# Second cross-attention: probabilities transposed on VectorE in 32x32 blocks, values as four row tiles

## The chip, the cores and the metric

The kernel runs on one core of a Trainium2 chip. The metric is the device time of one execution in microseconds, the median of several runs. Lower is better.

## What is computed

Two layers of a perceiver (cross-attention, self-attention, feed-forward) over x of 128 batches, 32 queries and 128 features, with a context of 128 x 257 x 128. The change touches only the second layer's cross-attention:

```python
Q = (queries @ W_Q).reshape(b, sq, H, DK)      # b=128, sq=32, H=16, DK=64
K = (keys @ W_K).reshape(b, skv, H, DK)        # skv=257; keys = values = context
V = (values @ W_V).reshape(b, skv, H, DV)
scores = jnp.einsum('bqhd,bkhd->bhqk', Q, K)
scores = jnp.where(mask == 0, -jnp.inf, scores)
probs = jax.nn.softmax(scores * scaling, axis=-1)
attn = jnp.einsum('bhqk,bkhd->bqhd', probs, V).reshape(b, sq, H * DV)
return attn @ W_O
```

All of it is in f32. The kernel folds W_Q with W_K into `A` and W_V with W_O into `BH` (`c_B` in the rows), so that scores and values work on the raw context of 128 features.

## The kernel before

The program is a chain of phases, each over all the data; `phase_xattn1` (line 755) is the one here, its tiles and buffers named `c_...`. Its main part takes one batch a step, 128 steps, and a tile is four batches (32 x 4 = 128 rows of x). The engines run the same steps, each with its own written order, coupled by semaphores; `run` (line 888) unrolls the first 8 steps, loops over eight at a time, and unrolls the last. r is the step modulo 8, and what depends on it does so modulo 4.

TensorE in step g (`step`, line 985):
- scores of batch g (L962): four matmuls of 257 keys, one for each group of four heads, into banks `b_s`;
- values of batch g-2 (L981): the probabilities, keys on the partitions (`PT`), times the context `C` (two halves of 128 keys), 512 columns each, into bank `b_o`;
- queries (L946) for the next tile, a quarter in each step, into bank `b_q`;
- at r%4 = 1 a small matmul of the last key's probabilities (L997); at r%4 = 2 the output projection of a tile, 16 matmuls (L1007) and one of 64 rows (L1009), into free columns of `b_s[0]`;
- the turn of batch g-1's probabilities (L970): eight transposes of 128x128 into two banks `b_pt`.

A matmul of f32 stands in the trace as two loads and two matmuls, a transpose as one of each.

ScalarE: the exponentials of batch g-1 (L1038, four, each followed by a read of the sum), eviction of the values (L1044, `OT`), eviction of the queries (L1026, `QP`), and eviction of the first half of the turned probabilities (L1051). VectorE: mask and maximum for each of four head groups (L1072), the reciprocal, scaling of the probabilities by it (L1082), at r%4 = 1 the small tile `LT` (L1087), at r%4 = 2 the addition to X (L1092), and the second half of the turned probabilities (L1098). GpSimd copies the last key's columns. SyncE loads for each batch the transposed context `cT` and the context rows `C`, eight buffers each.

Waits that the prediction follows: scores at r%4 = 0 wait for all four query evictions of their tile (`q_ev`); the second head group's scores at r%4 = 2 wait for `LT` to be made (`l_ev`), whose source lies in the same bank; the first group's at r%4 = 3 wait for the addition to X (`y_ev`), again for the bank's sake.

Of the kernel before, what the change touches and what calls it, by code (L numbers as in the profile page):

```python
# [754 lines left out]
def phase_xattn1(nc, sh, ctx_rows, mask, w_q, w_k, w_v, w_o):  # L755
# [7 lines left out]
    with ExitStack() as ctx:  # L763
# [8 lines left out]
        C = sb("c_C", [P, NC_, 2, D])  # L772
# [5 lines left out]
        PT = sb("c_PT", [P, 2, 2, 4, P])  # L778
# [8 lines left out]
        b_pt = [psum("c_bp0"), psum("c_bp1")]  # L787
        b_o, b_q = psum("c_bo"), psum("c_bq")

        with ExitStack() as prep:  # L790
# [15 lines left out]

            phase_norm(nc, sh, "c_n_", loads, b_pt)
# [68 lines left out]
        c_in = [sem(f"c_c_in{i}") for i in range(NC_)]  # L876
        ct_in = [sem(f"c_ct_in{i}") for i in range(NC_)]
        vb_in = [sem(f"c_vb_in{i}") for i in range(2)]
        taken, last_cp, bm_ok = sem("c_taken"), sem("c_last_cp"), sem("c_bm_ok")
        q_ps, q_ev = sem("c_q_ps"), sem("c_q_ev")  # L880
        s_ps, s_mx, s_nmx, e_ok = sem("c_s_ps"), sem("c_s_mx"), sem("c_s_nmx"), sem("c_e_ok")
        rd_ok, n_ok, x_ok = sem("c_rd_ok"), sem("c_n_ok"), sem("c_x_ok")
        pt_ps, pt0_ev, pt1_ev = sem("c_pt_ps"), sem("c_pt0_ev"), sem("c_pt1_ev")
# [57 lines left out]
        def _(pe):  # L941
            def queries(tile, c):
# [22 lines left out]
            def turn_probs(s, pair):  # L965
                wait(pe, n_ok, 4 * (s.g - 1) + 2 * pair + 2)
                wait(pe, (pt0_ev, pt1_ev)[pair], s.g - 1)
                for c in range(2):
                    for k in range(2):
                        last = nc.tensor.transpose(b_pt[pair][:, (2 * c + k) * P:(2 * c + k + 1) * P],  # L970
                                                   PR[:, 1 - s.r % 2, 2 * pair + k, c * P:(c + 1) * P], sh.ident[:, :])
                last.then_inc(pt_ps, 1)

            def values(s):
                g, buf = s.g, (s.r - 2) % NC_
                pe.wait_ge(c_in[buf], 16 * (s.eights(-2) + 1))
                wait(pe, pt0_ev, g - 1)
                wait(pe, pt1_ev, g - 1)
                wait(pe, o_ev, g - 2)
                for c in range(2):  # L980
                    last = nc.tensor.matmul(b_o[:, :], C[:, buf, c, :], PT[:, s.r % 2, c, :, :],  # L981
                                            start=(c == 0), stop=(c == 1))
                last.then_inc(av_ps, 1)

            def step(s):
                g, r = s.g, s.r
                if s.on(0):
                    scores(s)
                if s.on(2):
                    values(s)  # L990
                if s.on(-4):
                    queries(s.tile + 1, r % 4)
                if r % 4 == 1 and s.on(5):
                    wait(pe, x_ok, 4 * s.fours(-5) + 4)
                    if s.on(0):
                        wait(pe, s_mx, 4 * g + 2)
                    nc.tensor.matmul(b_s[1][0:BPT * H, SPARE:SPARE + SQ], XL[:, (r - 5) // 4 % 2, :, :, :],  # L997
                                     sh.fold[:, :], start=True, stop=True).then_inc(l_ps, 1)
                if r % 4 == 2 and s.on(6):
                    t, tp = s.fours(-6), (r - 6) // 4 % 2  # L1000
                    wait(pe, o_ev, 4 * t + 4)
                    wait(pe, l_ev, t + 1)
                    pe.wait_ge(vb_in[tp], 16 * (s.eights(-6) + 1))
                    if s.on(0):
                        wait(pe, s_mx, 4 * g + 1)
                    for h in range(H):
                        nc.tensor.matmul(b_s[0][:, SPARE:SPARE + D], OT[:, tp, h, :, :], BH[:, h, :],  # L1007
                                         start=(h == 0), stop=False)
                    nc.tensor.matmul(b_s[0][:, SPARE:SPARE + D], LT[:, :, :], VB[:, tp, :], start=False, stop=True  # L1009
                                     ).then_inc(y_ps, 1)  # L1010
                if s.on(1):
                    turn_probs(s, 0)
                    turn_probs(s, 1)

            for c in range(4):
                queries(0, c)
# [3 lines left out]
        def _(act):  # L1020
            nc.scalar.activation(warm[:, :], sh.ident[:, 0:1], ACT.Exp)

            def queries(tile, par, c):
# [3 lines left out]
                                     b_q[:, :].rearrange("p (h b q) -> p h b q", h=4, b=BPT), ACT.Copy  # L1027
                                     ).then_inc(q_ev, 1)

            def step(s):  # L1030
                g, r = s.g, s.r
                par = r % 2
                if s.on(1):
                    wait(act, s_nmx, g)
                    wait(act, pt_ps, 2 * (g - 2))
# [5 lines left out]
                if s.on(2):  # L1041
                    wait(act, av_ps, g - 1)
                    wait(act, y_ps, s.fours(-2) - 1)
                    nc.scalar.activation(OT[:, (r - 2) // 4 % 2, :, (r - 2) % 4, :],  # L1044
                                         b_o[:, :].rearrange("p (h q) -> p h q", h=H), ACT.Copy).then_inc(o_ev, 1)
                if s.on(-4):
                    queries(s.tile + 1, 1 - r // 4 % 2, r % 4)
                if s.on(1):
                    wait(act, pt_ps, 2 * (g - 1) + 1)
                    wait(act, av_ps, g - 2)  # L1050
                    nc.scalar.activation(PT[:, 1 - par, :, 0:2, :].rearrange("p c k q -> p c (k q)"),  # L1051
                                         b_pt[0][:, :].rearrange("p (c k) -> p c k", c=2), ACT.Copy).then_inc(pt0_ev, 1)
# [6 lines left out]
        def _(dve):  # L1059
# [4 lines left out]
            def step(s):  # L1064
# [12 lines left out]
                if s.on(1):  # L1077
# [17 lines left out]
                if s.on(1):  # L1095
                    wait(dve, pt_ps, 2 * g)
                    wait(dve, av_ps, g - 2)
                    nc.vector.tensor_copy(PT[:, 1 - par, :, 2:4, :].rearrange("p c k q -> p c (k q)"),  # L1098
                                          b_pt[1][:, :].rearrange("p (c k) -> p c k", c=2)).then_inc(pt1_ev, 1)
# [1349 lines left out]
```

## Time and profile before

| | us |
|---|---|
| median of 3 runs (2770.66 to 2772.89) | 2771.66 |
| profiled execution, time | 2771.93 |
| profiled execution, span | 2770.2 |
| scores of this phase, first to last start | 1068.2 to 1873.8 |

Over the whole span TensorE is busy 82% of the time, VectorE 60%, ScalarE 56%, GpSimd 17%. Busy shares of the whole span mix six phases; the phase in question is read in its own window. Durations in the rows are those of single instructions, and on TensorE successive ones overlap, so that what a group costs there is read from start to start of the groups.

### The profile page before, as it was taken

Reading aid. Unit: us, or ns where it says so; the run is one execution under the profiler, and the core shown is the slowest. Engines: PE = TensorE matmul, PEld = TensorE weight load, DVE = VectorE, ACT = ScalarE, POOL = GpSimd, SP = SyncE. Lnnn points to the kernel's source line nnn. Section 1 sums busy time; section 2 is a strip of 40 time slices with the busy share of each in tenths; the row PEclk is TensorE's granted clock in tenths of the full one; section 3 lists DMA queues with packets and bytes.
Section 4 is the critical chain, followed back from the end, with each engine's and each line's share of the span. In section 5 each row is a group of like instructions: output and inputs, shape, how many; then the busy total and the mean of one; then the engine's idle time right before and its main releaser. Section 6 shows DMA issues by size and latency. Waiting matters only on the chain. (4 is left out here: it accounts for less than half of the span.)

```text
span 2770.2 us, 66495 instructions
## 1 busy us (share of the span) xinstructions
PE 2272.8 (82%) x19392; PEld 1626.9 (59%) x19431; DVE 1654.2 (60%) x5152; ACT 1559.2 (56%) x3838; POOL 460.4 (17%) x1102
## 2 busy tenths in 40 slices
PE   5999999979669988999999999993455025399997
PEld 3777777757546666777778777772134013244443
DVE  5877887857454444666665666666889986611100
ACT  5888888867412234655655565553679457442221
POOL 2444445423113310000000000000000030000000
PEclk9999999989779988999999999997888555599999
DMA  3222222200100001111111111100000000000001
GB/s 90 74 74 71 75 74 70 74 15 0 25 0 0 0 33 62 48 42 42 41 45 43 37 47 41 43 27 31 0 1 0 0 2 3 21 22 0 0 0 31
DMA packets 153174, 90.36 MB, mean 33 GB/s; under 512 B 34032, under 2 KB 151168, under 8 KB 152704
## 3 DMA queue, kind: packets, MB, share of 16 engines
q1 hardware_dynamic: 153088, 89.26, 11.0%
q8 instruction: 49, 0.80, 0.1%
q14 instruction: 37, 0.30, 0.0%
HBM read 68.24 MB, written 20.97 MB: 32 GB/s over the span
## 5 line engine op out<-in xcount | busy, mean ns | idle before, releaser
L666 ACT ACTIVATE a_PR<-a_SM,a_nmx 128x257 f32<-128x257 f32 x512 | 253.3, 499 | 4.0 <-issue 3.3
L1038 ACT ACTIVATE c_PR<-c_SM,c_nmx 128x257 f32<-128x257 f32 x512 | 253.3, 501 | 0.0
L962 PE MATMUL c_bs<-c_cT,c_QP 128*128 128x257 f32 x1024 | 247.8, 385 | 0.8 <-ACT c_QP L1026 0.8
L981 PE MATMUL c_bo<-c_PT,c_C 128*128 128x512 f32 x512 | 240.7, 592 | 2.0 <-DVE c_PT L1098 2.0
L1072 DVE CUSTOM_DVE_ANT_0 c_SM<-c_bs,c_MB 128x257 f32<-128x257 f32 x512 | 215.1, 423 | 17.0 <-PE c_bs L962 14.2
L713 DVE CUSTOM_DVE_ANT_0 a_SM<-a_bs,a_MB 128x257 f32<-128x257 f32 x512 | 187.9, 422 | 44.5 <-PE a_bs L534 38.6
L962 PEld LDWEIGHTS c_bs<-c_cT,c_QP 128*128 128x128 f32 x1024 | 185.5, 191 | 26.3 <-issue 1.7
L946 PEld LDWEIGHTS c_bq<-c_XNT,c_A 128*128 128x128 f32 x1024 | 137.5, 196 | 67.3 <-issue 64.1
L1044 ACT ACTIVATE c_OT<-c_bo 128x512 f32<-128x512 f32 x128 | 76.5, 598 | 173.1 <-PE c_bo L981 173.1
L1098 DVE COPY c_PT<-c_bp 128x512 f32<-128x512 f32 x128 | 88.5, 691 | 121.4 <-PE c_bp L970 121.4
L933 POOL TENSOR_TENSOR c_XL<-quarter,c_PR 128x16 f32<-128x16 f32 x128 | 27.8, 218 | 774.1 <-DVE c_PR L1082 774.1
L1051 ACT ACTIVATE c_PT<-c_bp 128x512 f32<-128x512 f32 x128 | 76.0, 594 | 131.2 <-PE c_bp L970 131.1
L1082 DVE TENSOR_SCALAR c_PR<-c_PR,c_rden 128x257 f32<-128x257 f32 x512 | 146.2, 350 | 4.5
L946 PE MATMUL c_bq<-c_XNT,c_A 128*128 (+1 forms) x1024 | 139.0, 280 | 7.0 <-PEq L790 5.0
L2334 ACT ACTIVATE g_A<-g_b,g_S 128x512 f32<-128x512 f32 x64 | 44.0, 687 | 170.8 <-PE g_b L2298 170.8
L2366 DVE TENSOR_TENSOR g_YS<-g_b,g_s 128x512 f32<-128x512 f32 x8 | 5.5, 691 | 224.2 <-PE g_b L2323 224.2
L981 PEld LDWEIGHTS c_bo<-c_PT,c_C 128*128 128x128 f32 x512 | 97.1, 190 | 70.3 <-issue 63.6
L2067 PE MATMUL d_bv<-d_WQ,d_HQ 128*128 128x512 bf16 x33 | 20.7, 633 | 143.3 <-PEq L1942 115.2
L544 PE MATMUL a_bp<-ident,a_PR 128*128 128x128 f32 x1024 | 136.9, 276 | 1.7 <-ACT a_PR L666 1.4
L970 PE MATMUL c_bp<-ident,c_PR 128*128 128x128 f32 x1024 | 136.8, 276 | 0.9 <-DVE c_PR L1082 0.9
L1007 PE MATMUL c_bs<-c_B,c_OT 128*128 128x128 f32 x1024 | 119.7, 275 | 0.5 <-ACT c_OT L1044 0.5
L970 PEld LDWEIGHTS c_bp<-ident,c_PR 128*128 128x128 f32 x1024 | 112.7, 141 | 8.8 <-DVE c_PR L1082 3.4
(486 smaller groups left out, 5326.0 us busy)
## 6 DMA issues: line engine op xcount, KB each, us to landing
a_C<-in_ctx_dram SPq DMA_DIRECT2D x128, 128.0 KB, 2.1
ctxT_dram<-a_cT SPq DMA_DIRECT2D x128, 128.0 KB, 1.9
c_cT<-ctxT_dram SPq DMA_DIRECT2D x128, 128.0 KB, 2.2
c_C<-in_ctx_dram SPq DMA_DIRECT2D x128, 128.0 KB, 2.1
a_MK<-in_mask_Bx1xSxS_bk_dram SPq DMA_DIRECT2D x128, 32.1 KB, 1.9
X<-in_x_dram SPq DMA_DIRECT2D x4, 512.0 KB, 6.1
g_h<-in_L_ffn_h_w_dram SPq DMA_DIRECT2D x2, 1024.0 KB, 7.9
out_dram<-X SPq DMA_DIRECT2D x1, 2048.0 KB, 8.7
```

Of the source, the lines that this page charges most:

```text
L544: last = nc.tensor.transpose(b_pt[pair][:, (2 * k + c) * P:(2 * k + c + 1) * P], PR[:, par, 2 * pair + k, c * P:(c + 1) * P], sh.ident[:, :])
L666: nc.scalar.activation(PR[:, 1 - par, hg, :], SM[:, 1 - par, hg, :], ACT.Exp, bias=nmx[:, 1 - par, hg:hg + 1], accum_out=den[:, 1 - par, h ...
L713: nc.vector.tensor_tensor_reduce(SM[:, par, hg, :], b_s[hg][:, 0:SK], MB[:, par, :], 1.0, NEG1, ALU.add, ALU.max, mx[:, par, hg:hg + 1]).t ...
L946: last = nc.tensor.matmul(b_q[:, i * P:(i + 1) * P], A[:, 4 * c + i, :], sh.XNT[:, ds(tile * P, P)], start=True, stop=True)
L962: nc.tensor.matmul(b_s[hg][:, 0:SK], QP[:, r // 4 % 2, r % 4, 4 * hg:4 * hg + 4, :], cT[:, r, :], start=True, stop=True).then_inc(s_ps, 1)
L970: last = nc.tensor.transpose(b_pt[pair][:, (2 * c + k) * P:(2 * c + k + 1) * P], PR[:, 1 - s.r % 2, 2 * pair + k, c * P:(c + 1) * P], sh.i ...
L981: last = nc.tensor.matmul(b_o[:, :], C[:, buf, c, :], PT[:, s.r % 2, c, :, :], start=(c == 0), stop=(c == 1))
L1007: nc.tensor.matmul(b_s[0][:, SPARE:SPARE + D], OT[:, tp, h, :, :], BH[:, h, :], start=(h == 0), stop=False)
L1038: nc.scalar.activation(PR[:, 1 - par, hg, :], SM[:, 1 - par, hg, :], ACT.Exp, bias=nmx[:, 1 - par, hg:hg + 1], scale=SCALE, accum_out=den[ ...
L1072: nc.vector.tensor_tensor_reduce(SM[:, par, hg, :], b_s[hg][:, 0:SK], MB[:, :], 1.0, NEG1, ALU.add, ALU.max, mx[:, par, hg:hg + 1]).then_i ...
L1082: nc.vector.tensor_scalar(PR[:, 1 - par, hg, :], PR[:, 1 - par, hg, :], rden[:, 1 - par, hg:hg + 1], None, ALU.mult).then_inc(n_ok, 1)
L1098: nc.vector.tensor_copy(PT[:, 1 - par, :, 2:4, :].rearrange("p c k q -> p c (k q)"), b_pt[1][:, :].rearrange("p (c k) -> p c k", c=2)).the ...
```

## The change

The probabilities of a batch are no longer turned by TensorE. VectorE transposes them in blocks of 32x32 after it has scaled them (four instructions of 256 columns). A block transpose leaves head group h on partitions 32h to 32h+31, with 32 keys there, so the values become sums over 8 blocks of 32 keys, for each head group on its own 32 rows of the array: 32 matmuls of 32 rows and 128 columns, in place of two of 128 rows and 512 columns. Each needs its 32 context rows on the same partitions, so the context is loaded four times, once for each group of 32 partitions, into four buffers in place of eight. The values take four PSUM banks, one for each row tile; the queries move into other columns of these banks and are now computed before the values. The copies of turned probabilities on ScalarE and VectorE fall away. ScalarE's order of the rest, and the order of the engine's other work, stay.

```diff
-        C = sb("c_C", [P, NC_, 2, D])
+        C = sb("c_C", [P, NV, NKB, D])
...
-        PT = sb("c_PT", [P, 2, 2, 4, P])
+        PT = sb("c_PT", [P, 2, NKB, 4, SQ])
...
-        b_pt = [psum("c_bp0"), psum("c_bp1")]
-        b_o, b_q = psum("c_bo"), psum("c_bq")
+        b_o = psum("c_bo", (P, 4, 512))
...
-                wait(sp, av_ps, g - NC_ + 1)
-                sp.dma_start(C[:, r, :, :], ctx_rows[ds(g, 1), 0:LAST, :].rearrange("b (c p) d -> p (b c) d", p=P)
-                             ).then_inc(c_in[r], 16)
+                wait(sp, av_ps, g - NV + 1)
+                for h in range(4):
+                    sp.dma_start(C[32 * h:32 * h + 32, r % NV, :, :],
+                                 ctx_rows[ds(g, 1), 0:LAST, :].rearrange("b (c p) d -> p (b c) d", p=32)
+                                 ).then_inc(c_in[r % NV], 16)
...
                 wait(pe, q_ev, 4 * tile + c)
+                wait(pe, o_ev, o_done)
                 for i in range(4):
-                    last = nc.tensor.matmul(b_q[:, i * P:(i + 1) * P], A[:, 4 * c + i, :],
+                    last = nc.tensor.matmul(b_o[:, i, P:2 * P], A[:, 4 * c + i, :],
...
-            def turn_probs(s, pair):
...
+                wait(pe, t_ok, 4 * (g - 1))
                 wait(pe, o_ev, g - 2)
-                for c in range(2):
-                    last = nc.tensor.matmul(b_o[:, :], C[:, buf, c, :], PT[:, s.r % 2, c, :, :],
-                                            start=(c == 0), stop=(c == 1))
+                wait(pe, q_ev, g + 4 if s.on(-4) else B)
+                pe.sem_inc(taken_values, 1)
+                for kb in range(NKB):
+                    for h in range(4):
+                        rows = slice(32 * h, 32 * h + 32)
+                        last = nc.tensor.matmul(b_o[:, h, 0:P], C[rows, buf, kb, :], PT[rows, s.r % 2, kb, :, :],
+                                                start=(kb == 0), stop=(kb == NKB - 1), tile_position=(32 * h, 0))
                 last.then_inc(av_ps, 1)
...
+                if s.on(-4):
+                    queries(s.tile + 1, r % 4, g - 2)
                 if s.on(2):
                     values(s)
-                if s.on(-4):
-                    queries(s.tile + 1, r % 4)
...
-                if s.on(1):
-                    turn_probs(s, 0)
-                    turn_probs(s, 1)
...
+                    wait(dve, av_ps, g - 2)
+                    for hg in range(4):
+                        wait(dve, n_ok, 4 * (g - 1) + hg + 1)
+                        nc.vector.transpose(PT[:, 1 - par, :, hg, :], PR[:, 1 - par, hg, 0:LAST]).then_inc(t_ok, 1)
```

On TensorE, step r = 1 and the start of step 2 in the loop's first tile, before:

```order
L981 MATMUL c_bo<-c_PT,c_C 128x512 x2
L59 REGISTER_ALU
L946 MATMUL c_bq<-c_XNT,c_A 128x128 x4
L59 ISA x2
L997 MATMUL c_bs<-fold,c_XL 64x32
L970 MATMUL c_bp<-ident,c_PR 128x128 x8
L59 REGISTER_ALU x2
L962 MATMUL c_bs<-c_cT,c_QP 128x257 x2
```

and the same place of the change (its L968, L952 are the scores and the queries):

```order
L952 MATMUL c_bo<-c_XNT,c_A 128x128 x4
L59 REGISTER_ALU
L981 MATMUL c_bo<-c_PT,c_C 128x128 x32
L59 ISA x2
L997 MATMUL c_bs<-fold,c_XL 64x32
L59 REGISTER_ALU x2
L968 MATMUL c_bs<-c_cT,c_QP 128x257 x2
```

The queries stand ahead of the values, and nothing stands between the sums' matmul and the next scores, whose second half needs what VectorE makes of those sums. On VectorE the same step, before:

```order
L1082 TENSOR_SCALAR c_PR<-c_PR,c_rden 128x257 x4
L59 REGISTER_ALU x2
L1087 TENSOR_TENSOR c_LT<-c_bs,c_bmask 64x128
L59 REGISTER_ALU
L1098 COPY c_PT<-c_bp 128x2x256
```

and of the change:

```order
L1071 RECIPROCAL c_rden<-c_den 128x4
L1074 TENSOR_SCALAR c_PR<-c_PR,c_rden 128x257 x4
L1079 STREAM_TRANSPOSE c_PT<-c_PR 128x8x32 x4
L59 REGISTER_ALU x2
L1083 TENSOR_TENSOR c_LT<-c_bs,c_bmask 64x128
```

The four transposes stand between the scaling and `LT`, where before `LT` came first and the copy last. On ScalarE two steps, before:

```order
L1038 ACTIVATE c_PR,c_den<-c_SM,c_nmx 128x257 x4
L1044 ACTIVATE c_OT<-c_bo 128x16x32
L59 REGISTER_ALU
L1026 ACTIVATE c_QP<-c_bq 128x4x4x32
L59 ISA
L1051 ACTIVATE c_PT<-c_bp 128x2x256
```

and of the change:

```order
L1035 ACTIVATE c_PR,c_den<-c_SM,c_nmx 128x257 x4
L1041 ACTIVATE c_OT<-c_bo 128x4x4x32
L59 REGISTER_ALU
L1023 ACTIVATE c_QP<-c_bo 128x4x4x32
L59 REGISTER_ALU x2
```

The eviction of the queries still follows that of the values, though on TensorE they have changed places.

## Rows read from the trace of the kernel before

**Rows 1.** Windows: the loop of the phase; busy of PE, PEld, DVE, ACT, POOL; clock, DMA

```profile
1100.00:1820.00 720.00, 720.00 (x4174) 572.97 (x4173) 443.46 (x1778) 417.11 (x1240) 41.58 (x226) 1.00 0.15 42
```

**Rows 2.** Waits, 1100 to 1885: who waited for whom, us in total, times, longest

```profile
ACT c_OT L1044 <- PE c_bo L981: 167.6, 124, 2.9
...
DVE c_LT L1087 <- PE c_bs L997: 26.8, 30, 2.5
...
PE c_bo L981 <- DVE c_PT L1098: 2.0, 2, 1.0
```

**Rows 3.** Timeline of TensorE over one tile: start, length, engine, line, operation, count

```profile
1491.42 1.90 PE L962 MATMUL c_bs<-c_cT,c_QP 128*128 128x257 f32 x8
1493.15 1.88 PE L981 MATMUL c_bo<-c_PT,c_C 128*128 128x512 f32 x4
1494.87 1.05 PE L946 MATMUL c_bq<-c_XNT,c_A 128*128 x8
1495.76 1.04 PE L970 MATMUL c_bp<-ident,c_PR 128*128 128x128 f32 x8
1496.69 2.00 PE L962 MATMUL c_bs<-c_cT,c_QP 128*128 128x257 f32 x8
...
1501.13 1.04 PE L970 MATMUL c_bp<-ident,c_PR 128*128 128x128 f32 x8
1502.00 1.90 PE L962 MATMUL c_bs<-c_cT,c_QP 128*128 128x257 f32 x8
...
1515.61 0.48 PE L1009 MATMUL c_bs<-c_VB,c_LT 64*128 64x128 f32 x2
1516.03 1.09 PE L970 MATMUL c_bp<-ident,c_PR 128*128 128x128 f32 x8
1516.96 0.60 PE L962 MATMUL c_bs<-c_cT,c_QP 128*128 128x257 f32 x2
```

**Rows 4.** Timeline of ScalarE, end of that tile's first step and the next

```profile
1495.07 0.60 ACT L1044 ACTIVATE c_OT<-c_bo 128x512 f32<-128x512 f32 x1 [1.32 <-PE c_bo L981]
1495.96 0.60 ACT L1026 ACTIVATE c_QP<-c_bq 128x512 f32<-128x512 f32 x1 [0.29 <-PE c_bq L946]
1496.45 0.59 ACT L1051 ACTIVATE c_PT<-c_bp 128x512 f32<-128x512 f32 x1
1496.93 0.51 ACT L1038 ACTIVATE c_PR<-c_SM,c_nmx 128x257 f32<-128x257 f32 x1
...
1498.81 0.19 ACT L1038 ACTIVATION_READ_ACCUMULATOR c_PR<-c_SM,c_nmx 128x1 f32 x1
```

**Rows 5.** Timeline of VectorE in the same tile

```profile
1497.58 0.43 DVE L1072 CUSTOM_DVE_ANT_0 c_SM<-c_bs,c_MB 128x257 f32<-128x257 f32 x1
...
1499.62 1.14 DVE L1082 TENSOR_SCALAR c_PR<-c_PR,c_rden 128x257 f32<-128x257 f32 x4
...
1506.78 0.28 DVE L1087 TENSOR_TENSOR c_LT<-c_bs,c_bmask 64x128 f32<-64x128 f32 x1 [0.79 <-PE c_bs L997]
...
1516.25 0.29 DVE L1092 TENSOR_TENSOR X<-X,c_bs 128x128 f32 x1 [4.67 <-PE c_bs L1009]
```

**Rows 6.** First cross-attention: timeline of TensorE around its row tiles, and their durations (min/median/max)

```profile
404.13 0.44 PE L505 MATMUL a_bck<-ident,a_C 128*128 128x128 f32 x2
404.50 0.71 PE L534 MATMUL a_bs<-a_KT,a_Qb 32*128 32x257 f32 x8
405.14 0.48 PE L511 MATMUL a_bck<-a_cT,a_wk 128*128 128x256 f32 x1
...
L534 PEld LDWEIGHTS a_bs<-a_KT,a_Qb x1024: 181/183/185, 50.7 to 575.8; 32*128 32x128 f32 x171
L534 PE MATMUL a_bs<-a_KT,a_Qb x1024: 375/425/480, 50.7 to 576.0; 32*128 32x257 f32 x171
```

**Rows 7.** Groups of instructions: shapes, count | busy us, mean ns | idle before

```profile
L1082 DVE TENSOR_SCALAR c_PR<-c_PR,c_rden 128x257 f32<-128x257 f32 x512 | 146.2, 350 | 4.5
...
L2005 DVE STREAM_TRANSPOSE d_PT<-d_pb 128x2048 bf16<-128x2048 bf16 x8 | 18.5, 2311 | 0.3
```

**Rows 8.** Page, DMA queues: the fetches of TensorE's instructions, packets, MB, share

```profile
q8 instruction: 49, 0.80, 0.1%
```

More of the change, by code:

```diff
@@ L771, in phase_xattn1 @@
         SPARE = SK
-        C = sb("c_C", [P, NC_, 2, D])
+        NKB = LAST // 32
+        NV = 4
+        C = sb("c_C", [P, NV, NKB, D])
         cT = sb("c_cT", [D, NC_, SK])
@@ L805, in loads @@
                     sp.dma_start(MI[h * SQ:(h + 1) * SQ, :], mask[0, 0, :, :]).then_inc(m_in, 16)
+            b_pt = [b_o[:, 0, :], b_o[:, 1, :]]
             phase_norm(nc, sh, "c_n_", loads, b_pt)
@@ L874, in _ @@
                             m += 1
-        c_in = [sem(f"c_c_in{i}") for i in range(NC_)]
+        c_in = [sem(f"c_c_in{i}") for i in range(NV)]
         ct_in = [sem(f"c_ct_in{i}") for i in range(NC_)]
@@ L879, in phase_xattn1 @@
         taken, last_cp, bm_ok = sem("c_taken"), sem("c_last_cp"), sem("c_bm_ok")
+        taken_values = sem("c_taken_values")
         q_ps, q_ev = sem("c_q_ps"), sem("c_q_ev")
@@ L882, in phase_xattn1 @@
         rd_ok, n_ok, x_ok = sem("c_rd_ok"), sem("c_n_ok"), sem("c_x_ok")
-        pt_ps, pt0_ev, pt1_ev = sem("c_pt_ps"), sem("c_pt0_ev"), sem("c_pt1_ev")
+        t_ok = sem("c_t_ok")
         av_ps, o_ev, l_ps, l_ev = sem("c_av_ps"), sem("c_o_ev"), sem("c_l_ps"), sem("c_l_ev")
@@ L941, in _, with queries @@
         def _(pe):
-            def queries(tile, c):
+            def queries(tile, c, o_done):
                 wait(pe, q_ev, 4 * tile + c)
+                wait(pe, o_ev, o_done)
                 for i in range(4):
-                    last = nc.tensor.matmul(b_q[:, i * P:(i + 1) * P], A[:, 4 * c + i, :],
+                    last = nc.tensor.matmul(b_o[:, i, P:2 * P], A[:, 4 * c + i, :],
                                             sh.XNT[:, ds(tile * P, P)], start=True, stop=True)
@@ L963, in scores @@
                                      start=True, stop=True).then_inc(s_ps, 1)
-            def turn_probs(s, pair):
-                wait(pe, n_ok, 4 * (s.g - 1) + 2 * pair + 2)
-                wait(pe, (pt0_ev, pt1_ev)[pair], s.g - 1)
-                for c in range(2):
[L969 to L972, printed above, removed]
             def values(s):
[L975 to L978, printed above, removed]
+                g, buf = s.g, (s.r - 2) % NV
+                pe.wait_ge(c_in[buf], 64 * (s.fours(-2) + 1))
+                wait(pe, t_ok, 4 * (g - 1))
                 wait(pe, o_ev, g - 2)
-                for c in range(2):
-                    last = nc.tensor.matmul(b_o[:, :], C[:, buf, c, :], PT[:, s.r % 2, c, :, :],
-                                            start=(c == 0), stop=(c == 1))
+                wait(pe, q_ev, g + 4 if s.on(-4) else B)
[5 more added lines that the diff above has]
+                                                start=(kb == 0), stop=(kb == NKB - 1), tile_position=(32 * h, 0))
                 last.then_inc(av_ps, 1)
@@ L1010, in step @@
                                      ).then_inc(y_ps, 1)
-                if s.on(1):
-                    turn_probs(s, 0)
-                    turn_probs(s, 1)
             for c in range(4):
-                queries(0, c)
+                queries(0, c, 0)
             run(pe, step, 3)
@@ L1026, in queries @@
                 nc.scalar.activation(QP[:, par, :, 4 * c:4 * c + 4, :].rearrange("p b h q -> p h b q"),
-                                     b_q[:, :].rearrange("p (h b q) -> p h b q", h=4, b=BPT), ACT.Copy
+                                     b_o[:, :, P:2 * P].rearrange("p h (b q) -> p h b q", b=BPT), ACT.Copy
                                      ).then_inc(q_ev, 1)
@@ L1034, in step @@
                     wait(act, s_nmx, g)
-                    wait(act, pt_ps, 2 * (g - 2))
+                    wait(act, t_ok, 4 * (g - 2))
                     wait(act, x_ok, g - 2)
@@ L1043, in step @@
                     wait(act, y_ps, s.fours(-2) - 1)
-                    nc.scalar.activation(OT[:, (r - 2) // 4 % 2, :, (r - 2) % 4, :],
-                                         b_o[:, :].rearrange("p (h q) -> p h q", h=H), ACT.Copy).then_inc(o_ev, 1)
+                    nc.scalar.activation(OT[:, (r - 2) // 4 % 2, :, (r - 2) % 4, :].rearrange("p (a h) q -> p h a q", h=4),
+                                         b_o[:, :, 0:P].rearrange("p h (a q) -> p h a q", a=4), ACT.Copy).then_inc(o_ev, 1)
                 if s.on(-4):
                     queries(s.tile + 1, 1 - r // 4 % 2, r % 4)
[L1048 to L1052, printed above, removed]
             for c in range(4):
@@ L1094, in step @@
                     tile_stats(nc, dve, sh, t, y_ev, t + 1)
[L1095 to L1099, printed above, removed]
             run(dve, step, 3)
```

## The prediction, made before the changed kernel was run

> **What bounds the kernel now.** I read the windows view first: over 720 us of the phase's loop TensorE is busy 720.00 us at a granted clock of 1.00 (the 2.4 GHz level), while VectorE has 443.46 and ScalarE 417.11 [rows 1]. TensorE sets the pace and nothing else does. The waits agree: ScalarE waits 167.6 us in all for TensorE's values, VectorE 26.8 for the small sums' matmul, and TensorE itself waits for a copy only twice [rows 2]. So a step costs what stands on TensorE, and one tile of four steps is the unit: scores to scores four steps later, 1491.42 to 1516.96, 25.54 us [rows 3]. I call the steps r = 3, 0, 1, 2, as they stand in those rows. In each: scores 1.73 us (1491.42 to 1493.15), values 1.72 (to 1494.87), queries 0.89 (to 1495.76), turning the probabilities 0.93 (to 1496.69); the turn is 0.87 in step 0 (1501.13 to 1502.00).
>
> **What leaves TensorE.** Per tile four turns, 0.93 + 0.87 + 0.93 + 0.93 = 3.66 us (the last is 1516.03 to 1516.96; step 1's reads the same), and four times the old values, 6.88. Together 10.54 us.
>
> **What comes to TensorE.** 32 matmuls of 128 columns in four row tiles. The first cross-attention already runs such tiles: eight matmuls of 257 columns (two passes of four heads) take 0.71 us as a row, one lasts 0.375, so the last starts 0.335 after the first [rows 6]; one by one at 0.217 each (1.73 / 8) it would be 1.52. Four tiles stream at once. With 128 columns, eight full matmuls with a new weight load each take 1.05 us, 0.11 apart. I take 0.112 a round; 8 key blocks in 2 passes are 16 rounds, 1.79 us. Then the switch between full array and row tiles. The last full matmul at 404.13 + 0.44 - 0.27 = 404.30 is followed by the row tiles at 404.50: 0.20, where 0.11 is the usual step, and the first of them lasts 0.480 in place of 0.375 because its own load isn't hidden [rows 6]. That is 0.195 us; on the way out the same (405.14 is 0.305 after the last start, where 0.215 is streaming) plus 0.02, as the fourth tile starts later. Values new: 1.79 + 0.195 + 0.215 = 2.20 us, per tile 8.80. In step 1 the way out coincides with a switch that is there already (the 64-column sums matmul): -0.20. In steps 1 and 2 the scores now bear the load of 0.105 after such a switch: +0.21. So 8.81 come, 10.54 go: TensorE's own work falls by **1.73 us a tile**, 55 us in 32 tiles. That would be 2717.
>
> **What the removed turn was hiding.** Three results of other engines were made during the turn, and now the scores follow at once. This is where I put the case.
>
> Wait A, scores of step 0 on the queries' eviction. In each step ScalarE first evicts the values, then the queries; the queries are now computed before the values, but their eviction still queues behind the values' one, and scores of a new tile need all four. From the start V of the last round: its matmuls end at V + 0.02 + 0.27, ScalarE starts 0.04 later (values' row ends 1495.03 in its pattern, eviction at 1495.07 [rows 4]), the second eviction 0.49 after the first (1495.96 to 1496.45), and ends 0.60 later: V + 1.42. Scores start 0.13 after that (1496.56 to 1496.69), V + 1.55. Without a wait they would start at V + 0.11 + 0.215 = V + 0.32. Price **1.23 us**. Before, the eviction ended within the turn.
>
> Wait B, second head group of scores in step 2 on VectorE's LT. Count from the scores of step 0. VectorE starts the maxima at 0.22 + 0.38 + 0.04 = 0.64 and reaches the scaling 2.04 later (1497.58 to 1499.62 [rows 5]); four scalings 0.265 apart, then four transposes of T each. With T = 0.35 it is free at 5.14. TensorE starts step 1 at 1.73 + 0.89 + 0.195 + 1.79 + 0.215 = 4.82. ScalarE evicts values at 4.83, queries at 5.32, starts the exponentials 0.48 later (1496.45 to 1496.93) and has all four after 2.07 (to 1499.00): 7.87. VectorE scales from 8.11, transposes from 9.17 to 10.57, makes LT in 0.28 [rows 5] to 10.85, and the matmul follows 0.13 later, 10.98. TensorE is there at 4.82 + 4.60 + 0.43 for the sums matmul and its switches + 0.43 for the first head group = 10.28. Price **0.70 us**; it grows by 4T.
>
> Wait C, scores of step 3 on the addition to X, whose PSUM bank they share. The last output matmul ends 1516.09; the addition runs 1516.25 to 1516.54 [rows 3, 5], scores could start at 1516.67. Unhindered they would start where the turn's first matmul really streams, 1516.03 + 0.055, plus 0.05 for a longer load: 1516.13. Price **0.54 us**. The copy of the turned half used to come after it.
>
> Sum: -1.73 + 1.23 + 0.70 + 0.54 = **+0.74 us a tile**, times 32 = +24 us on the profiled execution's 2771.93 us, which is 0.27 above the median of the three runs. Forecast 2796.
>
> **The price of a transpose.** No 32-bit transpose is in the trace. The nearest row is one of 2048 bf16 columns, 2311 ns; scaled by columns that is 0.29 us for 256. The scaling of 257 columns lasts 350 ns [rows 7] at 0.265 spacing, so at that pace 2048 columns take 2.11 us and 0.20 of the 2311 is fixed: 0.46 lasting, some 0.38 apart. I take 0.35. The lower end is 0.265 (as the scaling), the upper 0.58 (should a 4-byte element cost two 2-byte ones, 2 x 0.29). Wait B makes that 2785 and, with 4 x 0.23 x 32 = 29 more, 2825. The Trainium skill, "Vector Engine (DVE) Microarchitecture Reference", section 3.8, has the 32x32 reorder array sustain one element per cycle and lane; with the 1.04 ns of its section 5.2 that is an estimate of 0.27 us, and the sum would be 2785. It doesn't say that this holds for 4 bytes, and no row here shows it.
>
> **What costs nothing.** VectorE loses the copy of 0.69 and gains four transposes, 1.4: its step grows to about 5.1 us against 4.8 to 10 on TensorE, fed by tiles with slack in step 2. ScalarE loses a copy of 0.6. The context now comes four times: three more DMAs of 128 KB a step, 61 MB more; at a DMA share of 0.15 for two such transfers [rows 1] five need about 0.37. Only four buffers are left in place of eight, so SyncE waits for the values four batches back before it sends the next batch's keys; these are needed more than two steps, 10 us, later and land in about 2. If one came late, each step would pay it.
>
> **Rivals.**
> 1. *The waits are covered.* If wait B vanishes (transposes early, exponentials not behind the evictions), +0.04 a tile, 2773: no change, 0.11. If wait A vanishes, -0.49 a tile, -16 us, 2756; all three, 2717. The queries' eviction would have to end 0.19 after the last round starts; the order written for ScalarE puts it at 1.42. Together 0.11 for faster.
> 2. *Transposes twice as long*, 2825; for it only that the trace has 2-byte ones alone. 0.08.
> 3. *The loop's code is refetched.* TensorE's loop grows from 180 to 356 matmuls, nearly all issued as two loads and two passes. Its instruction pages are fetched 49 times in the whole run [rows 8], which is once per page, so today's loops are never fetched again. If the longer body doesn't stay resident, each of 15 backward jumps waits for a page, about 2 us as a transfer lands: up to +30, 2826. Part would fall into wait A. 0.05. The Trainium skill, "Runtime: NRT & Kernel Launch", section "Instruction fetch mechanics", says a taken branch out of the resident window forces such a fetch.
> 4. *Row tiles don't overlap their loads in a long run.* A load lasts 0.183 [rows 6]; load and stream in turn, 0.29 a round, would add 2.85 a step, over 3100. The eight in [rows 6] load the second round under the first, but only once. 0.03.
>
> **How the numbers follow.** The forecast case has 0.62 and spans 2783 to 2812 (T from 0.265 to 0.48, round from 0.107 to 0.12). A measurement of this kernel tells 0.2%, 5.5 us, from no change. Slower: 0.62 + 0.08 + 0.05 + 0.03 = 0.78; same 0.11; faster 0.11. The range 2768 to 2830 leaves out the faster cases and the failed overlap, and a part of 2 and 3: under 0.2.
>
> **What would show it.** Right: TensorE's busy share in the loop falls from 100% to about 90; its waits name the queries' eviction with 1.2 us x 32, LT with 0.7 and X with 0.5; the values' group takes 1.9 to 2.0 us a batch; a tile takes 26.3 us. Wrong: no such waits (then 2717), values of 4 us or more (rival 4), transposes over 0.5 us (rival 2), more than 59 instruction pages of 16 KB (rival 3).

## The result, and the profile after

| | before | after |
|---|---|---|
| median, us | 2772.27 (2770.66 to 2773.80) | 2796.21 (2795.30 to 2799.28) |
| profiled execution, time | 2771.93 | 2795.99 |
| profiled execution, span | 2770.2 | 2794.2 |
| scores of the phase, first to last start | 1068.2 to 1873.8 | 1067.7 to 1898.1 |

Each is the median of 4 runs; the ratio is 1.0088, 95% interval 1.0071 to 1.0106. The change makes the kernel slower by 24 us, and all of it lies in the phase: from first to last start of the scores it takes 830.4 us in place of 805.6. The forecast was 2796, slower. A tile, the unit of the prediction, is counted here from the scores of one r = 3 step to the next.

In the changed kernel the scores are L968, the queries L952, the values L981, the small sums L997, the output projection L1007 and L1009. Windows view of the loop, as [rows 1] (PE, PEld, DVE, ACT, POOL, then clock, DMA share, GB/s):

```profile
1100.00:1820.00 720.00, 655.18 (x9701) 586.51 (x9694) 502.46 (x2035) 331.68 (x1090) 39.97 (x218) 1.00 0.40 101
```

TensorE, busy all of the time before, is now busy 91% of it, at the same clock of 1.00. What it waits for is in the view of the waits, 1100 to 1905, as [rows 2] (us in total, times, longest):

```profile
ACT c_OT L1041 <- PE c_bo L981: 436.0, 123, 6.6
DVE c_SM L1064 <- PE c_bs L968: 92.5, 117, 1.7
PE c_bs L968 <- ACT c_QP L1023: 38.9, 30, 1.4
PE c_bs L968 <- DVE X L1088: 17.8, 31, 0.6
PE c_bs L968 <- DVE c_LT L1083: 16.0, 30, 1.3
PE c_bo L981 <- DVE c_PT L1079: 1.5, 1, 1.5
```

Three waits of TensorE's scores, once a tile each, 72.7 us together: the queries' eviction (A), LT (B), the addition to X (C). The values wait for transposed probabilities once in this window, at the end of the phase. VectorE and ScalarE still wait for TensorE as well: neither is full. The timeline of TensorE over one tile, as [rows 3]:

```profile
1502.33 1.97 PE L968 MATMUL c_bs<-c_cT,c_QP 128*128 128x257 f32 x8 [0.59 <-DVE X L1088]
1504.14 1.05 PE L952 MATMUL c_bo<-c_XNT,c_A 128*128 x8
1505.12 2.07 PE L981 MATMUL c_bo<-c_PT,c_C 32*128 32x128 f32 x64
1508.47 2.00 PE L968 MATMUL c_bs<-c_cT,c_QP 128*128 128x257 f32 x8 [1.28 <-ACT c_QP L1023]
1510.30 1.05 PE L952 MATMUL c_bo<-c_XNT,c_A 128*128 x8
1511.29 2.07 PE L981 MATMUL c_bo<-c_PT,c_C 32*128 32x128 f32 x64
1513.28 2.00 PE L968 MATMUL c_bs<-c_cT,c_QP 128*128 128x257 f32 x8
1515.12 1.05 PE L952 MATMUL c_bo<-c_XNT,c_A 128*128 x8
1516.10 2.07 PE L981 MATMUL c_bo<-c_PT,c_C 32*128 32x128 f32 x64
1518.10 0.30 PE L997 MATMUL c_bs<-fold,c_XL 128*64 128x32 f32 x2
1518.33 0.70 PE L968 MATMUL c_bs<-c_cT,c_QP 128*128 128x257 f32 x2
1519.49 1.54 PE L968 MATMUL c_bs<-c_cT,c_QP 128*128 128x257 f32 x6 [0.46 <-DVE c_LT L1083]
1520.87 1.05 PE L952 MATMUL c_bo<-c_XNT,c_A 128*128 x8
1521.85 2.07 PE L981 MATMUL c_bo<-c_PT,c_C 32*128 32x128 f32 x64
1523.85 3.84 PE L1007 MATMUL c_bs<-c_B,c_OT 128*128 128x128 f32 x32
1527.62 0.48 PE L1009 MATMUL c_bs<-c_VB,c_LT 64*128 64x128 f32 x2
```

The next scores start at 1528.69, so this tile takes 26.36 us, 0.82 more than before. The loop does two tiles a round, and the starts of the scores show that they alternate between 26.36 and 26.47 (before: 25.54 and 25.56); the mean of a pair is 0.87 more than before. Values undisturbed take 2.00 us to the next group (1521.85 to 1523.85); between the steps r = 3 and r = 0 it is 3.35 (1505.12 to 1508.47), and the difference, 1.35, is wait A. ScalarE behind those values, as [rows 4]:

```profile
1507.25 0.60 ACT L1041 ACTIVATE c_OT<-c_bo 128x512 f32<-128x512 f32 x1 [6.51 <-PE c_bo L981]
1507.75 0.59 ACT L1023 ACTIVATE c_QP<-c_bo 128x512 f32<-128x512 f32 x1
1508.22 0.51 ACT L1035 ACTIVATE c_PR<-c_SM,c_nmx 128x257 f32<-128x257 f32 x1
```

The second eviction ends 1508.34 and the scores start 0.13 later, with queries that TensorE had finished at 1505.2. VectorE's transposes have their group in the lines view, as [rows 7]:

```profile
L1079 DVE STREAM_TRANSPOSE c_PT<-c_PR 128x256 f32<-128x256 f32 x512 | 181.3, 412 | 0.0
```

### The profile page after: what moved, and what is told of

Read it like the earlier page. It is cut to its first block and busy times, and to the rows that moved or that the text cites. A ratio compares the mean times of both kernels' runs of the same rounds, so it can differ in the third digit from the quotient of the medians.

```text
span 2794.2 us, 80685 instructions
## 1 busy us (share of the span) xinstructions
PE 2235.6 (80%) x26087; PEld 1664.0 (60%) x26087; DVE 1742.5 (62%) x5536; ACT 1474.9 (53%) x3710; POOL 459.9 (16%) x1102
## 3 DMA queue, kind: packets, MB, share of 16 engines
q1 hardware_dynamic: 257536, 139.61, 18.9%
## 5 line engine op out<-in xcount | busy, mean ns | idle before, releaser
L968 PE MATMUL c_bs<-c_cT,c_QP 128*128 128x257 f32 x1024 | 263.9, 396 | 75.3 <-ACT c_QP L1023 41.1
L981 PE MATMUL c_bo<-c_PT,c_C 32*128 32x128 f32 x8192 | 264.5, 276 | 3.6 <-DVE c_PT L1079 3.4
L968 PEld LDWEIGHTS c_bs<-c_cT,c_QP 128*128 128x128 f32 x1024 | 182.5, 190 | 122.2 <-issue 97.9
L981 PEld LDWEIGHTS c_bo<-c_PT,c_C 32*128 32x128 f32 x8192 | 240.2, 186 | 19.9 <-issue 5.4
L1079 DVE STREAM_TRANSPOSE c_PT<-c_PR 128x256 f32<-128x256 f32 x512 | 181.3, 412 | 0.0
L952 PEld LDWEIGHTS c_bo<-c_XNT,c_A 128*128 128x128 f32 x1024 | 137.5, 196 | 15.5 <-issue 5.8
L952 PE MATMUL c_bo<-c_XNT,c_A 128*128 (+1 forms) x1024 | 139.0, 280 | 7.0 <-PEq L791 5.0
L2058 PE MATMUL d_bv<-d_WQ,d_HQ 128*128 128x512 bf16 x64 | 33.1, 621 | 131.0 <-PEq L1933 114.9
L1007 PE MATMUL c_bs<-c_B,c_OT 128*128 128x128 f32 x1024 | 122.8, 278 | 0.5 <-ACT c_OT L1041 0.5
L1007 PEld LDWEIGHTS c_bs<-c_B,c_OT 128*128 128x128 f32 x1024 | 116.7, 192 | 4.3 <-ACT c_OT L1041 0.6
L544 PEld LDWEIGHTS a_bp<-ident,a_PR 128*128 128x128 f32 x1024 | 112.8, 141 | 8.1 <-ACT a_PR L666 3.1
L2289 PE MATMUL g_b<-g_A,g_H1T 128*128 128x512 f32 x256 | 111.3, 592 | 1.6 <-DVE g_A L2352 1.6
```

What stands on the lines that cost most here:

```text
L544: last = nc.tensor.transpose(b_pt[pair][:, (2 * k + c) * P:(2 * k + c + 1) * P], PR[:, par, 2 * pair + k, c * P:(c + 1) * P], sh.ident[:, :])
L952: last = nc.tensor.matmul(b_o[:, i, P:2 * P], A[:, 4 * c + i, :], sh.XNT[:, ds(tile * P, P)], start=True, stop=True)
L968: nc.tensor.matmul(b_s[hg][:, 0:SK], QP[:, r // 4 % 2, r % 4, 4 * hg:4 * hg + 4, :], cT[:, r, :], start=True, stop=True).then_inc(s_ps, 1)
L981: last = nc.tensor.matmul(b_o[:, h, 0:P], C[rows, buf, kb, :], PT[rows, s.r % 2, kb, :, :], start=(kb == 0), stop=(kb == NKB - 1), tile_po ...
L1079: nc.vector.transpose(PT[:, 1 - par, :, hg, :], PR[:, 1 - par, hg, 0:LAST]).then_inc(t_ok, 1)
L2289: last = nc.tensor.matmul(b_h[m % 2][:, :], hT[:, kb, m * P:(m + 1) * P], src[:, kb, :], start=(kb == 0), stop=(kb == KB - 1))
```

## The experiments

My theory: TensorE's own work fell by some 55 us as reckoned, and the waits A, B and C, which the turn of the probabilities used to cover, give back more than that. The rival: the loss is the price of row tiles, of fourfold loads or of a loaded VectorE, and the waits only mark where TensorE would be held anyway. The timed runs beside their forecasts (each ratio is to the kernel before, timed in the same session; "all three" are the first three changes together):

| kernel | median, us | ratio, 95% interval | against after (2796.2) |
|---|---|---|---|
| queries a step ahead | 2755.3 | 0.9937 (0.9920 to 0.9954) | -40.9 |
| LT first | 2779.3 | 1.0016 (1.0005 to 1.0027) | -16.9 |
| output projection first | 2772.0 | 0.9997 (0.9988 to 1.0006) | -24.2 |
| all three | 2711.8 | 0.9781 (0.9761 to 0.9801) | -84.4 |
| before, three more loads a step | 2772.5 | 0.9997 (0.9988 to 1.0006) | |
| transposes twice | 2859.9 | 1.0313 (1.0299 to 1.0327) | +63.7 |
| all three, six blocks | 2653.9 | 0.9576 (0.9562 to 0.9591) | |
| all three, transposes twice | 2757.3 | 0.9943 (0.9930 to 0.9957) | |
| all three, values in pairs | 2759.6 | 0.9948 (0.9934 to 0.9961) | |
| pairs with mended orders | 2708.6 | 0.9764 (0.9751 to 0.9778) | -87.6 |

### Queries a step ahead: wait A

```diff
-                if s.on(-4):
-                    queries(s.tile + 1, r % 4, g - 2)
+                if s.on(-5):
+                    queries(s.fours(5), (r + 1) % 4, g - 2)
```

ScalarE's evictions and the bank's wait follow by the same shift.

> The changed kernel with the queries computed and evicted one step earlier (each quarter five steps ahead of its use in place of four, one more quarter ahead of the loop); nothing else moves. My theory: the scores of step 0 then find all four evictions done, wait A (1.30 us x 30 in the trace of the changed kernel, 39 us with the unrolled steps) goes, waits B and C stay: 2796 - 39 = 2757 us. Rival (the waits only stand where TensorE would be held anyway, by the context's transfers or by VectorE): another wait takes its place and the time stays at 2790 to 2796.

Measured 2755.3. The trace has no wait for the queries' eviction left, and B and C stand as they were:

```profile
PE c_bs L968 <- DVE X L1090: 17.8, 31, 0.6
PE c_bs L968 <- DVE c_LT L1085: 16.0, 30, 1.3
```

So the wait is worth what it shows, and nothing takes its place. With this one move the changed kernel is 0.6% faster than the kernel before.

### LT ahead of the transposes: wait B

```diff
+                if r % 4 == 1 and s.on(5):
+                    ... (LT)
                 if s.on(1):
                     wait(dve, av_ps, g - 2)
                     for hg in range(4):
                         ... (transposes)
-                if r % 4 == 1 and s.on(5):
-                    ... (LT)
```

> The changed kernel with LT made ahead of the four transposes on VectorE; nothing else moves. My theory: wait B (0.53 us x 30) goes, the transposes come 0.3 us or so later and are not needed before the values of the next step, 2.6 us on: 2796 - 16 = 2780 us. Rival (VectorE itself is late, so that the later transposes hold the values): no gain, 2796, with a wait of the values for the transposes.

Measured 2779.3, 16.9 less. The scores' wait for LT is gone, and the values find their transposes in time though these now come later. The mean tile is 0.62 us shorter, where the view of the waits counts 0.53 for this wait: the view counts idle time, and the price is the distance between starts.

### Output projection ahead of the values: wait C

```diff
                 if s.on(-4):
                     queries(s.tile + 1, r % 4, g - 2)
+                if r % 4 == 2 and s.on(6):
+                    ... (L1007, L1009)
                 if s.on(2):
                     values(s)
-                if r % 4 == 2 and s.on(6):
-                    ... (L1007, L1009)
```

> The changed kernel with the output projection (16 matmuls and the one of 64 rows) issued after the queries and ahead of the values in its step; nothing else moves. My theory: the addition to X then runs under the values, wait C (0.57 us x 31, 18 us) goes: 2796 - 18 = 2778 us. Against it: the addition stands behind the transposes on VectorE, and if these are late the wait stays; then 2796.

Measured 2772.0: 24.2 less, 6 more than expected. The timeline (its L999 and L1001 are the output projection; in the changed kernel they are L1007 and L1009) shows both parts:

```profile
1511.02 1.05 PE L952 MATMUL c_bo<-c_XNT,c_A 128*128 x8
1511.91 3.74 PE L999 MATMUL c_bs<-c_B,c_OT 128*128 128x128 f32 x32
1515.58 0.48 PE L1001 MATMUL c_bs<-c_VB,c_LT 64*128 64x128 f32 x2
1515.99 2.07 PE L981 MATMUL c_bo<-c_PT,c_C 32*128 32x128 f32 x64
1517.99 2.00 PE L968 MATMUL c_bs<-c_cT,c_QP 128*128 128x257 f32 x8
```

From L1001 to the next group it is 0.41 in place of 1.07: the wait cost 0.66 a tile, where the view of the waits counts 0.57. And the order saves a switch: queries to projection 0.89 (queries to values 0.98), projection 3.67 (3.77 behind row tiles). 0.66 + 0.09 + 0.10 = 0.85, times 29 to 31 is 25 to 26 us.

### All three

> The changed kernel with all three moves (queries a step ahead, LT ahead of the transposes, output projection ahead of the values). My theory: only TensorE's own work is left, which the prediction had 1.73 us a tile below the kernel before, 55 us: 2772 - 55 = 2717 us, and up to 8 us more for what is left between; faster than both kernels. Rival (row tiles, switches or the fourfold loads cost more than reckoned, the waits were only part of it): 2740 or more.

Measured 2711.8, 84.4 under the changed kernel, where the three apart make 82.0: the waits are independent. In the phase alone, from first to last start of the scores, the three runs are 43.7, 20.0 and 25.2 us under the changed kernel, 88.9 together, and this one is 88.1 under it. Some 6 us of that is the switch that the projection's new place saves; the rest is the waits, more than three times the 24 us that the change had lost. Its window, and the first and last line of one tile:

```profile
1100.00:1780.00 680.00, 680.00 (x10273) 616.98 (x10275) 521.84 (x2157) 350.10 (x1150) 42.20 (x230) 1.00 0.45 113
```

```profile
1482.86 2.00 PE L968 MATMUL c_bs<-c_cT,c_QP 128*128 128x257 f32 x8
...
1506.54 2.00 PE L968 MATMUL c_bs<-c_cT,c_QP 128*128 128x257 f32 x8
```

TensorE is busy all of the window again. This tile takes 23.68 us, its neighbours 23.57, 23.62 on the mean. The kernel is faster than both others: 2.2% under the one before.

### The loads by themselves

```diff
                              ).then_inc(c_in[r], 16)
+                wait(sp, ex_in[r % 4], 48 * s.fours(0))
+                for h in range(1, 4):
+                    sp.dma_start(EX[32 * h:32 * h + 32, r % 4, :, :],
+                                 ctx_rows[ds(g, 1), 0:LAST, :].rearrange("b (c p) d -> p (b c) d", p=32)
+                                 ).then_inc(ex_in[r % 4], 16)
```

> The kernel before with three more transfers of the context rows in each step, 32 partitions each as the changed kernel has them, into a buffer that nobody reads. My theory (the prediction's nothing for the transfers): 2772, within 4 us. Rival (part of the change's loss is contention of the DMA engines with the keys' transfers or with the engines for SBUF): 2780 or more.

Measured 2772.5, ratio 0.9997. The traffic is that of the changed kernel (139.61 MB on this queue in both, 89.26 before), and TensorE stays full:

```profile
1100.00:1820.00 720.00, 720.00 (x4169) 572.80 (x4169) 444.31 (x1779) 417.89 (x1242) 41.23 (x224) 1.00 0.38 104
```

So the fourfold load costs the kernel before nothing, and the kernel with the three moves, which has it too, keeps TensorE full.

### Transposes twice, in the changed kernel

```diff
+                    wait(dve, du_ok, 4 * (g - 1))
                     for hg in range(4):
                         wait(dve, n_ok, 4 * (g - 1) + hg + 1)
+                        nc.vector.transpose(DU[:, :, hg, :], PR[:, 1 - par, hg, 0:LAST]).then_inc(du_ok, 1)
+                    wait(dve, av_ps, g - 2)
+                    for hg in range(4):
                         nc.vector.transpose(PT[:, 1 - par, :, hg, :], PR[:, 1 - par, hg, 0:LAST]).then_inc(t_ok, 1)
```

> The changed kernel with four more transposes a step on VectorE, into a buffer that nobody reads, ahead of the real ones. My theory (wait B is VectorE's chain, and grows with the time of the four transposes): at 0.337 us each 1.35 us a tile at least, 40 us, 2836; and since the chain holds step 0's transposes too, whose slack before the next scores is only some 0.3 to 0.5 us, up to 0.9 us a tile more, 2862. Rival (VectorE, 62% busy over the span, takes them in its idle time): under 2806.

Measured 2859.9. In an ordinary tile the scores' third matmul waits from 1525.31 to 1527.95 (its scores are L969):

```profile
1525.31 0.70 PE L969 MATMUL c_bs<-c_cT,c_QP 128*128 128x257 f32 x2
1527.95 1.54 PE L969 MATMUL c_bs<-c_cT,c_QP 128*128 128x257 f32 x6 [1.93 <-DVE c_LT L1087]
```

That is 2.64 us in place of 1.16 and 1.25 in turn, 1.43 more on the mean where four transposes are 1.35; a tile takes 27.83 (1537.15 to 1564.98), 1.42 more than the mean of the changed kernel, 44 us in 31 tiles. Wait B is VectorE's chain, nearly one for one. But 64 were measured, and of the 0.9 a tile that I had kept for step 0's slack hardly 0.1 is there. The rest is something else. In 9 of 31 tiles, every third or fourth, the wait is followed by this:

```profile
1297.87 0.70 PE L969 MATMUL c_bs<-c_cT,c_QP 128*128 128x257 f32 x2
1300.50 1.98 PE L969 MATMUL c_bs<-c_cT,c_QP 128*128 128x257 f32 x6 [1.92 <-DVE c_LT L1087]
1302.27 1.92 PE L953 MATMUL c_bo<-c_XNT,c_A 128*128 x8
1304.12 2.40 PE L982 MATMUL c_bo<-c_PT,c_C 32*128 32x128 f32 x64
```

and the windows view there has the granted clock (third number, for 1300 to 1305) at 0.66, a mixture of the 1.2 and the 2.4 GHz level:

```profile
1295.00:1300.00 5.00, 3.57 (x75) 1.00 0.56 143
1300.00:1305.00 5.00, 4.50 (x30) 0.66 0.35 83
1305.00:1310.00 5.00, 5.00 (x87) 1.00 0.40 107
```

Eight query matmuls last 1.92 there in place of 1.05, and such a tile takes 29.4 us, 1.6 more than its neighbours: 9 x 1.6 = 14 us. Together 58 of the 62 us by which the phase is longer (892.5 in place of 830.4); the other 4 lie in its first and last steps, where the first such wait is 3.3 us. That the wait brings the fall of the clock is read from their order in time, here and at the end of the last kernel below; no run changes the length of a wait and nothing else.

### Transposes twice, with the waits gone

> The three moves together with the four transposes done twice. In the trace of the three moves VectorE is busy 4.55 us a batch and a batch takes 5.92; with 1.35 us more it is busy 5.90, the whole batch. My theory: the transposes that are there cost nothing once the waits are gone, and the second set costs only what VectorE lacks, 0.1 to 0.5 us a batch: 2725 to 2775, far under the 40 us and more that it costs the changed kernel. Rival (a transpose costs its time wherever it stands, by VectorE's port or by PSUM): 2711.8 + 4 x 0.337 x 128 = 2884.

Measured 2757.3, 45.5 above the three moves. VectorE (the third pair of columns) is now busy 637 of 700 us, and TensorE waits for its maxima, ahead of the output projection:

```profile
1100.00:1800.00 700.00, 674.34 (x9987) 604.28 (x9981) 637.38 (x2556) 342.40 (x1125) 41.56 (x226) 1.00 0.42 107
```

```profile
1502.98 3.84 PE L1000 MATMUL c_bs<-c_B,c_OT 128*128 128x128 f32 x32 [0.44 <-DVE c_mx L1067]
```

This is 0.44 a tile, and about as much stands ahead of one group of values, where the profile names no releaser. A tile takes 24.9 in place of 23.6 for 5.4 us more of VectorE: three quarters of the second set went into slack. The first set lies wholly in that slack: without the second, TensorE is full. The rival's 2884 is far off.

### Six blocks of keys: the price of a round

```diff
-                for kb in range(NKB):
+                for kb in range(6):
```

> The three moves together, with the values summed over six of the eight blocks of 32 keys (64 keys are left out of the values); it measures the price of a round of four row tiles. My theory: 4 rounds of 0.112 us less in each of 128 batches, 57 us under the 2711.8 of the three moves: 2654. Rival (the values are held by the switch, the loads or another engine, not by the number of rounds): 2680 or more.

Measured 2653.9, 57.9 under the three moves, which this kernel has too (it leaves out 64 of the 256 keys in the values); the values' group goes from 2.00 to 1.55 us (1501.61 to 1503.16):

```profile
1501.61 1.62 PE L981 MATMUL c_bo<-c_PT,c_C 32*128 32x128 f32 x48
1503.16 2.00 PE L968 MATMUL c_bs<-c_cT,c_QP 128*128 128x257 f32 x8
```

Four rounds are 0.45 us, 0.113 each. At this pace the loads must be hidden: a load alone lasts 0.187 in the changed kernel, and load and stream in turn had been put at 0.29.

### Values in pairs: the price of a switch

```diff
-                if s.on(2):
+                if s.on(2) and r % 2 == 1:
                     values(s)
...
+                for two in range(2):
+                    buf = (s.r - 3 + two) % NV
+                    for kb in range(NKB):
+                        ...
+                                matmul(b_o[:, h, 2 * P * two:2 * P * two + P], C[rows, buf, kb, :],
+                                       PT[rows, buf, kb, :, :], ...
```

> The three moves together, and the values of two batches one behind the other in every second step (32 rounds of four row tiles without a break, columns 0 to 127 and 256 to 383 of the four banks, four buffers of turned probabilities in place of two). It measures what entering and leaving the row tiles costs: a tile has two such pairs in place of four. My theory (0.195 in and 0.215 out, less the usual step of 0.11, by the prediction's terms; the second batch's rounds follow at 0.112): two pairs fewer are 0.6 to 0.8 us a tile, 19 to 26 us under the 2711.8 of the three moves: 2686 to 2693. Rival (the gap is not the switch's but waits that the profile doesn't name, or VectorE, at 77% busy, can't follow the uneven steps): 2712 or more.

Measured 2759.6, 48 above the three moves where 19 to 26 less was forecast: the forecast failed, but the price can be read.

```profile
1512.18 2.00 PE L968 MATMUL c_bs<-c_cT,c_QP 128*128 128x257 f32 x8
1514.10 1.15 PE L952 MATMUL c_bo<-c_XNT,c_A 128*128 x8
1515.88 2.00 PE L968 MATMUL c_bs<-c_cT,c_QP 128*128 128x257 f32 x8 [0.62 <-DMA c_cT<-ctxT_dram]
1517.71 1.05 PE L952 MATMUL c_bo<-c_XNT,c_A 128*128 x8
1518.99 3.85 PE L984 MATMUL c_bo<-c_PT,c_C 32*128 32x128 f32 x128 [0.23 <-issue]
1522.77 0.30 PE L1013 MATMUL c_bs<-fold,c_XL 128*64 128x32 f32 x2
```

128 matmuls take 3.78 us, two groups of 64 took 4.00. With the entry (0.98 in place of 0.89) one pair of switches, in and out, is about 0.3 us beyond the stream. The gain of two pairs a tile was overpaid by new waits: a tile takes 25.05. One wait is telling: SyncE sends the keys of the next batch behind the context rows, whose buffer now comes free a step later with only four of them, and the keys are late by 0.62 us, once a tile. The four buffers, which cost the changed kernel nothing, have no cover left here.

The last kernel mends the orders: keys ahead of the rows on SyncE, output projection ahead of the queries, LT again behind the transposes, exponentials of two batches ahead of both evictions.

> The paired values again, with the orders around them changed where the trace of the pair shows a wait: SyncE sends the keys of batch g+1 ahead of the context rows of batch g (the keys came late, 0.62 us a tile); the output projection stands ahead of the queries in its step (the addition to X then runs under the queries); LT is again behind the transposes; ScalarE does the exponentials of two batches in the odd steps, ahead of the evictions of the two values. My theory (the pair saves 0.30 us for each switch pair, 0.60 a tile, since its 128 matmuls took 3.81 us to the next group in place of 2 x 2.00 and the entry costs 0.095; the rest of the loss was waits): 2711.8 - 19 = 2693 us, up to 2700 with small waits left. Rival (the engines cannot follow the uneven steps whatever the order): 2712 or more, with waits of the scores or the values for VectorE.

Measured 2708.6, 3 us under the three moves, which is within the spread of either kernel's runs; 19 had been forecast. TensorE's waits for the keys, LT and X are gone, but for one. Tiles of 23.37 (1503.60 to 1526.97) and 23.49 us alternate, on the mean 0.19 under the three moves, where I had 0.60; 0.24 to 0.3 of the missing part is a late start of one of the two values' groups, for which the profile names no releaser, and the rest is open. Nor do the 6 us that 0.19 a tile makes all show: the first three tiles take 0.5 more than those of the three moves and the last one 2.6 more (23.60 for 21.02), of which 1.6 stand in the length of one group of values:

```profile
1795.84 5.48 PE L989 MATMUL c_bo<-c_PT,c_C 32*128 32x128 f32 x128 [2.07 <-issue]
```

```profile
1795.00:1800.00 5.00, 4.16 (x88) 0.66 0.12 21
```

Elsewhere in this kernel its 128 matmuls last 3.85 us; here, behind the wait of 2.07 us the granted clock is 0.66 on the mean, as in the doubled transposes. From first to last scores 3.5 us are left.

## Why the prediction was right, step by step

**TensorE's own work.** Without its waits (A 1.35, B 0.62, C 0.66) the mean tile of after is 26.41 - 2.63 = 23.78 us; 25.54 - 1.73 = 23.81 was forecast, and the kernel with the three moves takes 23.62, with 0.19 of it saved by the projection's place. The sum is right, but its parts are divided otherwise. The first full matmul after a switch starts 0.22 behind the last round, 0.11 beyond the usual step, and not 0.215 beyond it. The other 0.105 of the way out is that matmul's own weight load: it lasts 0.484 in place of 0.380, which doesn't delay its start but shows in the scores of the step, 1.83 for 1.73. A step r = 0 takes 4.81 (1508.47 to 1513.28), forecast 4.82. A round, taken as 0.112 from full matmuls [rows 3], measured 0.112 to 0.113, so rival 4 is out.

**Wait A**, forecast 1.23, is 1.35 by the timeline, and its run gave 41 us. ScalarE's chain was right: the last round starts at 1506.90, the scores 1.57 later, forecast 1.55. But without the wait they would start 0.22 after that round, not 0.32: the same weight load of 0.105, placed ahead of the start.

**Wait B**, forecast 0.70, is 0.62: the third matmul starts 1.16 after the first (1.25 in every other tile), and 0.54 (0.63) in the kernel with the three moves. The chain was right to 0.04 in the tile shown (third matmul 11.02 us after the scores of step 0, forecast 10.98) and to 0.14 in its neighbour; TensorE arrives later than reckoned, its first head group taking 0.54 or 0.63 in place of 0.43.

**Wait C**, forecast 0.54, is 0.66, with its switch.

**T**, taken as 0.35, is 0.337: four starts from 1506.30 to 1507.31, 1.01 us for three steps. One lasts 404 ns (the median; the mean in the row above is 412), the scaling of 257 columns 350. The Trainium skill, "Vector Engine (DVE) Microarchitecture Reference", section 3.8, has one element per cycle and lane, from which, with the 1.04 ns of its section 5.2, I had estimated 0.27. The measured 0.337 is a quarter above that, and decides; by 0.27 wait B would have been 0.3 smaller. The estimate had left out the 75 ns an instruction that the same section 5.2 of the Trainium skill puts on top; with them it would have been an estimate of 0.34. The scalings, 0.265 apart, don't show such a part, and with one length of f32 transposes in the runs it is open whether the transpose pays by the instruction or by the column.

**Sum.** Forecast +0.74 a tile, measured +0.87 on the mean: A +0.12, B -0.08, C +0.12 and TensorE's own work -0.03 against the forecast. That would be 27 us and not 24. The first three steps of the phase make up for it: the turn is gone there and the waits haven't begun, so they take 12.0 us in place of 14.4, and the 31 tiles behind them, the last one with +1.3, take 27.1 more. The prediction multiplied a full tile by 32 and left the two ends out. The mechanism was forecast; the agreement to the microsecond is luck.

**The rest.** ScalarE's and VectorE's work, the loads (DMA share 0.40 where 0.37 was reckoned) and four buffers cost nothing, as said. Three of the numbers on the way were wrong without moving the sum: the loads bring 50 MB more (139.61 for 89.26, as 3 x 128 KB x 128 gives) and not 61; VectorE's step, put at 5.1 us, has 4.6 of busy time (502.46 of 720 us, a quarter of 26.41); and the loop has 14 rounds, so 13 backward jumps and not 15. Rival 1 (waits covered) was the neighbour that lay nearest: its all-three case was put at 2717, and moving three steps gives 2712. Rival 2 needed 0.58 a transpose, measured 0.337. Rival 3 would show in the fetches:

```profile
q8 instruction: 58, 0.95, 0.1%
```

58 is under the 59 that I had named, and the trace has none of these fetches between 1155 and 1853 us, which covers all rounds of the loop but part of the first. The Trainium skill, "Runtime: NRT & Kernel Launch", section "Instruction fetch mechanics", has a window of two pages, of 256 instructions each, out of which a taken branch must fetch. TensorE's loop is longer (356 matmuls, nearly all issued as two loads and two passes, some 1400 instructions) and fetched nothing, so here the trace speaks against that rule. By the same section of the Trainium skill TensorE's instruction memory holds 2048 instructions, and with that figure the trace agrees.

## What to carry to other kernels

Before work is taken off the engine that sets the pace, list what its neighbours do under that work: each wait that ended inside the removed piece comes back, as far as it reaches past the new start, and the waits together can cost more than the piece was worth. Here the cure was the order, not the operation: produce a step earlier what is waited for, and put the short answer that the pace-setter needs ahead of the long work that nobody waits for. A wait read in the timeline (start to start, against the same group undisturbed) was its price here, and the idle time in the view of the waits fell 0.05 to 0.09 us short of it. The three separate waits on one engine added up. And where a loop's rounds hold two tiles, compare means of two.

## What the runs showed of the hardware

Four f32 block transposes of 128x256 start 0.337 us apart, against 0.265 for a scaling of 257 columns. Entering and leaving four row tiles costs about 0.3 us beyond the stream, with 48, 64 or 128 matmuls between as the trace counts them (1.55, 2.00 and 3.78 us to the next group, less 0.112 a round, and 0.09 at the entry). And the granted clock: with waits of up to 1.4 us of TensorE in the changed kernel it stays at 1.00, the 2.4 GHz level, through the whole loop; with waits of 1.9 us (transposes twice; 2.6 in the first tile) it is at the 1.2 GHz level behind the wait in 9 of 31 tiles, and in the others, after the same wait, it is not. I had not expected that a wait could be paid again in this way: here by 14 of the 64 us that doubling the transposes cost. The last kernel, with waits of 2.07 and 2.41 us at the end of its phase, has the clock at that level behind both; no wait of up to 1.7 us in the phase (values in pairs) was followed by it. What decides in which tiles it falls the runs don't show.
